# Wavelet attention and mixture of experts on one core: expert 0, the last experts and the shared expert's pieces in another order

## The chip, the cores and the metric

The kernel runs on one core of a Trainium2 chip. The metric is the device time of one execution in microseconds. Five engines work side by side and meet only at semaphores: TensorE (PE; its weight loads are PEld), VectorE (DVE), ScalarE (ACT), GpSimd (POOL) and SyncE (SP), which issues direct DMAs. GpSimd issues the indirect DMAs, gathers and scatters of rows by a list of indices.

## The reference, cut to what matters

Two sequences of 1024 tokens with 128 channels pass a wavelet block with linear attention, and then a mixture of experts:

```python
x = x + attention_block(layernorm(x))           # (2, 1024, 128)
h = layernorm(x).reshape(2048, 128)
scores = sigmoid(h @ gate_w.T)                  # 16 experts
topk_score, topk_ids = top_k(scores.T, 256)     # each expert takes its 256 best tokens
xin = h[topk_ids]
eo = silu(xin @ gw.T + gb) * (xin @ up_w.T + up_b)   # 512 hidden features
eo = eo @ down_w.T + down_b
out = zeros.at[topk_ids].add(eo * topk_score)
shared = (silu(h @ sh_gate_w.T) * (h @ sh_up_w.T)) @ sh_down_w.T   # 256 hidden features
x = x + out + shared
```

## The kernel before, in words

The order of the work is written out by hand, one program for each engine. Nothing plans it at run time: an engine executes its list in order, and each wait on a semaphore stops everything behind it in that list.

**The search.** For each expert the kernel needs the 256th largest score. It finds it in 15 rounds of a search over the bits of the scores (`ROUNDS`). In a round VectorE counts the keys above two candidates (L964), ScalarE those above a third with a Sign (`count_third`, L687), TensorE sums the three counts over partitions (`count`, L1318 to L1322), and VectorE reads the sum (L975) and lays the next candidates (L978). The next round starts from there.

**The shared expert** fills the engines beside the search. Its tokens come in four groups of 512 (`LAST` is group 3). For each group TensorE transposes the features (`features_T`, L1285), multiplies them with four weight tiles (`shared_up`, L1331, gate and up, two each) and, later, multiplies the hidden values with the down weights in four quarters (`shared_down`, L1343, four matmul pairs each group, 16 matmuls of 128 columns in all). ScalarE takes the gate through Silu and copies the up values (`keep_shared`, L700 and L695), copies the transposed features (`keep_hT`, L659) and the down results (`keep_down`, L680). GpSimd multiplies the two halves (L525) and adds the down result of group 0 to `x1` (`shared_add`, L515). Before the change, which piece stands in which round follows from the round's number by a rule, five rounds a group (`PERIOD`): TensorE does a `shared_up` in parts 0 to 3 of a group, with a `shared_down` quarter of the group before, and six warm-up matmuls in part 4; features are transposed in rounds 1, 7 and 11. ScalarE follows one round later (`keep_part`). `stay_warm(n)` issues n matmuls of the identity (L1145), in fp32 two passes each, whose results nobody reads. ScalarE's first Silu stands in round 1, and the compiler puts a load of the activation table ahead of it.

**After the search** the masks become ranks, and VectorE and TensorE turn these into row numbers for four groups of experts: 0 and 1, 2 and 3, 4 to 7 and, `LATE`, 8 to 15. The pieces of the late group's table (`LATER`) are laid between the tiles of the first experts on VectorE. `slot_rows` lets GpSimd gather.

**The experts.** `BLOCKS` lists them: experts 0 to 13 whole (256 tokens, two chunks of 128), experts 14 and 15 in two half blocks each (`HALVED = E - 2`). For step q of block b, with part j of the hidden features (`FT` is 4), TensorE multiplies with the up and the gate weights (L1488 and L1489, an "up" below, two passes each); ScalarE takes the gate through Silu (L745); VectorE makes the hidden tile (L1122); and TensorE multiplies the hidden tile with the down weights (`down`, L1457) two steps later (`LAG`). A block's last down lets VectorE add the bias (`add_bias`, L1104), then ScalarE scale the rows (`weigh`, L571), then GpSimd scatter them (`scatter`, L549). `turn_x` (L1443) transposes the gathered rows of a block, and VectorE copies them (`keep_x`, L1088). For whole blocks the next block's turn stands at part 2 of the block before, while blocks from `HALVED` on are turned late, after the last downs of the block before, with a few warm-ups between (`WARM_B`).

**The order on GpSimd** is fixed: 12 gathers ahead (`AHEAD`), then for each expert two scatters and, after them, two gathers (experts 0 to 5) or one (6 to 13) (`BETWEEN`). Chunk c of the gathers belongs to expert c // 2; so the gather behind expert 9's scatters is expert 13's second, the one behind expert 11's is expert 14's second. An expert's first scatter waits until both scatters of the expert before have landed:

```python
pool.wait_ge(s_scat, 16 * CH * e)      # for e == 0: s_store, the four stores of x1
```

Those stores are issued by SyncE (L399) as soon as a group of `x1` holds the shared expert's part. Group 3's part is added on VectorE by `add_shared(LAST, ...)` (L1055), which needs `shared_down(LAST, ...)`.

**Around expert 0, before.** TensorE's list is: up 0, the row numbers of experts 4 to 7 (`spread(2)`), up 1, `shared_down(LAST)` in four quarters into bank 6, up 2, down 0, turn 1, a wait until bank 6 is read, up 3, down 1, up 4, downs 2 and 3, up 5, up 6, down 4, turn 2, up 7, down 5, up 8. VectorE adds the shared part at step 2, and expert 0's bias at step 4; ScalarE scales expert 0 at step 4.

## Time and profile before

| what | before |
|---|---|
| median of 3 runs | 205.61 us (205.59 to 206.11) |
| the profiled execution | 205.9 us |
| its span, first to last instruction | 204.1 us |
| mean granted TensorE clock | 0.986 of full speed |
| busy: PE, DVE, POOL, ACT | 90%, 64%, 62%, 46% of the span |

The busy shares are averages over stages with different limits. The span is what lies between the first and the last instruction; the execution's own time is 1.8 us longer. In the rows below a time is the start of an instruction in microseconds from the span's start, followed by its duration. "x4" is a merged run of four instructions of one line. In brackets is how long the engine had been idle before, and what ended the idle time; "issue" means that it waited for nothing that the profile shows.

### The profile page before, as it was taken

How to read it: one execution, taken by the hardware profiler on the slowest of the kernel's cores; microseconds unless marked ns; L12 is line 12 of the kernel's file. 1: busy time of each engine (PE TensorE's matmuls, PEld its weight loads, DVE VectorE, ACT ScalarE, POOL GpSimd, SP SyncE). 2: the span in 40 equal slices, each digit the busy share in tenths (PEclk: the TensorE clock that was granted, in tenths of full speed). 3: DMA queues.
4: the chain of work that ended last, by engine and by line, in shares of the span. 5: the costliest groups of instructions: out<-in, count | busy, mean ns of one | idle time of the engine just before them, and what ended most of it. 6: DMA issues, size and time to landing. Idle time of an engine off the chain costs nothing.

```text
span 204.1 us, 3777 instructions
## 1 busy us (share of the span) xinstructions
PE 182.7 (90%) x1246; PEld 157.1 (77%) x1246; DVE 130.3 (64%) x452; ACT 94.2 (46%) x248; POOL 127.3 (62%) x195
## 2 busy tenths in 40 slices
PE   6989889999979999998999999999999979888830
PEld 6957679998936577845998999999999968777720
DVE  4888999999778787887566745544554443434420
ACT  2566612468697768120244244444444442444410
POOL 7598006455117475647766887888877778777550
PEclk9999999999999999999999999999999999999995
DMA  5799999700030271203413322432332233333311
GB/s 173 252 413 419 410 420 412 302 0 3 0 117 0 94 231 51 67 18 109 114 39 51 33 43 42 57 43 35 52 38 33 38 43 40 40 40 39 33 13 13
DMA packets 11652, 22.30 MB, mean 109 GB/s; under 512 B 1504, under 2 KB 8800, under 8 KB 11504
## 3 DMA queue, kind: packets, MB, share of 16 engines
q1 hardware_dynamic: 5968, 17.52, 22.6%
q0 software_dynamic: 5664, 4.53, 16.1%
q8 instruction: 10, 0.16, 0.3%
q14 instruction: 10, 0.08, 0.1%
HBM read 17.72 MB, written 4.33 MB: 108 GB/s over the span
## 4 chain that ended last, share of the span: by engine, by line
PE 38%; POOL 16%; DMA 14%; DVE 12%; issue 10%; ACT 5%; POOLq 1%; SPq 0%; DVEq 0%; ACTq 0%
DMA out_dram<-area,rows 13%; POOL out_dram L549 11%; PE bank L1190 7%; PE bank L1488 4%; PE bank L1331 4%; PE bank L1489 4%; POOL hT L538 3%; PE bank L1457 3%; PE bank L1145 3%; PE bank L1343 2%; POOL rstd L454 2%; DMA x_tok<-in_x_dram 2%; PE bank L1401 1%; PE bank L1293 1%; DVE junk L964 1%
## 5 line engine op out<-in xcount | busy, mean ns | idle before, releaser
L549 POOL DMA_INDIRECT out_dram<-area,rows x32 | 50.6, 1581 | 17.8 <-DMA out_dram<-area,rows 7.2
L1122 DVE SCALAR_TENSOR_TENSOR area<-bank,consts,sgate 128x256 f32<-128x256 f32 (+1 forms) x72 | 32.7, 454 | 44.8 <-ACT sgate L745 44.0
L745 ACT ACTIVATE sgate<-bank,consts 128x256 f32<-128x256 f32 (+1 forms) x72 | 32.4, 450 | 54.8 <-PE bank L1489 54.0
L1488 PE MATMUL bank<-area,wT 128*128 128x256 f32 (+1 forms) x144 | 40.4, 363 | 2.6 <-issue 2.5
L1457 PEld LDWEIGHTS bank<-wT,area 128*128 128x128 f32 x256 | 37.9, 191 | 6.0 <-DVE area L1122 2.7
L1457 PE MATMUL bank<-wT,area 128*128 128x128 f32 x256 | 40.2, 278 | 1.8 <-DVE area L1122 1.8
L538 POOL DMA_INDIRECT hT<-h_rows,rows x32 | 31.7, 991 | 13.3 <-issue 9.2
L1489 PE MATMUL bank<-area,wT 128*128 128x256 f32 (+1 forms) x144 | 39.5, 356 | 0.0
L1489 PEld LDWEIGHTS bank<-area,wT 128*128 128x128 f32 x144 | 26.1, 190 | 2.9
L1488 PEld LDWEIGHTS bank<-area,wT 128*128 128x128 f32 x144 | 21.9, 191 | 4.0 <-issue 3.8
L525 POOL TENSOR_TENSOR sh_hid<-sh_up,sgate 128x64 f32<-128x64 f32 x48 | 13.6, 322 | 15.0 <-ACT sh_up L695 12.4
L1145 PE MATMUL bank<-ident 128*128 128x128 f32 x132 | 19.9, 308 | 1.6 <-POOL ident L418 1.6
L1145 PEld LDWEIGHTS bank<-ident 128*128 128x128 f32 x132 | 18.4, 220 | 1.6 <-POOL ident L418 1.6
L1190 PE MATMUL bank<-sh_hid,area 128*128 128x128 f32 x160 | 18.6, 276 | 0.0
L1190 PEld LDWEIGHTS bank<-sh_hid,area 128*128 128x128 f32 x160 | 18.2, 192 | 0.3 <-ACT area L618 0.3
L1331 PE MATMUL bank<-hT,sh_wT 128*128 128x512 f32 x32 | 17.6, 636 | 0.6 <-ACT hT L659 0.6
L571 ACT ACTIVATE area<-area,hT 128x128 f32<-128x128 f32 x32 | 11.2, 392 | 7.9 <-DVE area L1104 7.9
L964 DVE TENSOR_SCALAR_CACHE_REDUCE junk<-area,search 128x256 bf16<-128x256 f32 (+1 forms) x30 | 13.2, 477 | 1.3 <-ACT area L673 0.8
L1343 PEld LDWEIGHTS bank<-sh_wT,sh_hid 128*128 128x128 f32 x64 | 8.5, 191 | 4.1 <-issue 2.9
L454 POOL TENSOR_TENSOR rstd<-var_eps,half_pow 128x4 f32<-128x4 f32 (+1 forms) x6 | 7.4, 1230 | 6.1 <-DVE var_eps L775 6.1
L498 POOL TENSOR_TENSOR x_tok<-x_tok,consts 128x128 f32<-128x128 f32 x4 | 3.1, 814 | 12.4 <-DVE area L887 12.4
L687 ACT ACTIVATE below<-area,search 128x256 bf16<-128x256 f32 (+1 forms) x15 | 7.6, 509 | 4.8 <-DVE search L978 4.0
(197 smaller groups left out, 265.5 us busy)
## 6 DMA issues: line engine op xcount, KB each, us to landing
wT<-in_weights_dram SPq DMA_DIRECT2D x16, 768.0 KB, 16.5
h_rows<-hrow SPq DMA_DIRECT2D x2, 576.0 KB, 3.7
x_tok<-in_x_dram SPq DMA_DIRECT2D x4, 256.0 KB, 3.6
x_tok<-in_down_b_dram SPq DMA_DIRECT2D x1, 1024.0 KB, 6.4
out_dram<-x SPq DMA_DIRECT2D x4, 256.0 KB, 2.2
hT<-h_rows,rows POOLq DMA_INDIRECT x32, 2.6
out_dram<-area,rows POOLq DMA_INDIRECT x32, 3.3
sh_wT<-in_shared_dram SPq DMA_DIRECT2D x1, 384.0 KB, 3.0
```

What stands on the lines that cost most here:

```text
L525: last = pool.tensor_tensor(sh_hid[:, n % 2, t, k:k + 64], sh_up[:, t, k:k + 64], sgate[:, t, k:k + 64], ALU.mult)
L538: pool.indirect_dma_start(out=gath[:, e % GBUF, c, :], out_offset=None, in_=h_rows[:, :], in_offset=bass.IndirectOffsetOnAxis(ap=rows[:, c ...
L549: pool.indirect_dma_start(out=out_rows, in_=eo[:, e % EOB, c, :], in_offset=None, out_offset=bass.IndirectOffsetOnAxis(ap=rows[:, c, e:e + ...
L745: act.activation(sgate_e[:, q % SGB, 0:n], up_bank(q)[:, CAP:CAP + n], ACT.Silu, bias=biasT[:, 1, j, e:e + 1]).then_inc(s_sil, 1)
L964: last = dve.tensor_scalar(junk[:, k, :], keys, cand[:, k:k + 1], 0.0, ALU.is_ge, ALU.add, accum_out=cnt[:, k:k + 1])
L1122: dve.scalar_tensor_tensor(hidden[:, b % 2, j, 0:n], up_bank(q)[:, 0:n], biasT[:, 0, j, e:e + 1], sgate_e[:, q % SGB, 0:n], ALU.add, ALU.m ...
L1145: pe.matmul(spare[:, 0:P], ident[:, :], ident[:, :], start=True, stop=True)
L1190: last = pe.matmul(dst, band[:, b, m0 + o:m0 + o + P], diag_c[:, d0 - 4 + k, :], start=False, stop=(d0 == 4 and o == 2), skip_group_check= ...
L1331: pe.matmul(bank[2 * kind + t][:, :], sh_wT[:, 2 * kind + t, :], rhs, start=True, stop=True).then_inc((s_shg, s_shu)[kind], 1)
L1457: last = pe.matmul(bank[3 + b % 2][:, i * P:(i + 1) * P], hidden[:, b % 2, j, i * P:(i + 1) * P], wT[:, e, 2, j, :], start=(j == 0 and i = ...
L1488: pe.matmul(up_bank(q)[:, 0:n], wT[:, e, 0, j, :], xselT[:, b % 2, 0:n], start=True, stop=True)
L1489: pe.matmul(up_bank(q)[:, CAP:CAP + n], wT[:, e, 1, j, :], xselT[:, b % 2, 0:n], start=True, stop=True).then_inc(s_gu, 1)
```

## The change

`HALVED` becomes E - 1: expert 14 is a whole block and only expert 15 is halved. A new constant, `TURN_LATE`, keeps the late turn, the late bias add and the late scaling for blocks from 14 on. The warm-ups ahead of the late blocks are now five before expert 14 and none before the two halves of expert 15; before, they were two ahead of each of the last three half blocks.

Expert 0's last three downs are issued at step 3. Group 3's `shared_down` moves from ahead of up 2 to a place between down 1 and down 2 and goes to bank 4; VectorE adds it at the end of step 3, directly ahead of expert 0's bias, and ScalarE scales expert 0 at step 3, ahead of the Silu of step 4.

In the search, tables by round take the place of the rule. TensorE's first `shared_up` stands in round 1, and no round holds more than one `shared_up` with one other piece. ScalarE's first Silu of the shared expert moves to round 2, and an 8-column Silu into a new tile `idle` stands in round 1. Warm-ups in the search are 15 in seven rounds, where they were 18 in three.

```diff
-    HALVED = E - 2
+    HALVED = E - 1
+    TURN_LATE = E - 2
+        idle = sb("idle", [P, 8])
         ROUNDS = [b for b in range(BITS - LOW - 2, -1, -2)] + [b for b in range(LOW - 2, -1, -2)]
         PERIOD = 5
+        ACT_PARTS = {2: (0, 0), 3: (0, 1), 4: (0, 2), 5: (0, 3), 6: (1, 0), 7: (1, 1), 8: (1, 2), 9: (1, 3),
+                     11: (2, 0), 12: (2, 1), 13: (2, 2), 14: (2, 3)}
+        UP_PARTS = {1: (0, 0, 0), 2: (0, 0, 1), 3: (0, 1, 0), 4: (0, 1, 1), 5: (1, 0, 0), 6: (1, 0, 1), 7: (1, 1, 0),
+                    8: (1, 1, 1), 10: (2, 0, 0), 11: (2, 0, 1), 12: (2, 1, 0), 13: (2, 1, 1)}
+        DOWN_PARTS = {7: ((0, 0),), 8: ((0, 1),), 9: ((0, 2), (0, 3)), 11: ((1, 0),), 12: ((1, 1),), 13: ((1, 2),),
+                      14: ((1, 3),)}
+        TURN_PARTS = {2: 1, 5: 2, 10: 3}
+        WARM_PARTS = {0: 3, 1: 2, 3: 2, 4: 2, 6: 2, 9: 1, 14: 3}
...
-        WARM_B = {HALVED + 1: 2, HALVED + 2: 2, HALVED + 3: 2}
+        WARM_B = {TURN_LATE: 5}
...
# ScalarE, round r of the search
-                if r:
-                    keep_part(r - 1)
-                if r == 2:
-                    keep_hT(1)
+                if r == 1:
+                    act.activation(idle[:, :], ident[:, 0:8], ACT.Silu)
+                if r in ACT_PARTS:
+                    keep_shared(*ACT_PARTS[r])
+                if r == 3:
+                    keep_hT(1)
+                if r == 10:
+                    keep_down(0)
...
-            keep_part(len(ROUNDS) - 1)
+            keep_down(1)
...
# ScalarE, step q of the experts
-                if b >= HALVED and j == 0:
+                if b >= TURN_LATE and j == 0:
                     weigh(act, b - 1)
...
-                if q == FT or j == 2 and 1 < b < HALVED:
+                if q == FT - 1:
+                    weigh(act, 0)
+                elif j == 2 and 1 < b < TURN_LATE:
                     weigh(act, b - 1)
...
# VectorE, step q
-                if q == 2:
-                    add_shared(LAST, bank[6])
-                if b >= HALVED and j == 0:
+                if b >= TURN_LATE and j == 0:
...
-                if q == FT or j == 1 and 1 < b < HALVED:
+                if q == FT - 1:
+                    add_shared(LAST, bank[4])
+                    add_bias(0)
+                elif j == 1 and 1 < b < TURN_LATE:
                     add_bias(b - 1)
...
# TensorE, shared_down of the last group
                 else:
                     pe.wait_ge(s_lasthid, SHT)
+                    pe.wait_ge(s_lastbase, 1)
...
# TensorE, round r
-                n, part = divmod(r, PERIOD)
-                if n < LAST and part < 4:
-                    shared_up(n, part // 2, part % 2)
-                    if n:
-                        shared_down(n - 1, part)
-                if part == 4:
-                    stay_warm(WARM_S, bank[6 + n % 2])
-                if r in (1, 7, 11):
-                    features_T(1 + r // 4)
+                if r in UP_PARTS:
+                    shared_up(*UP_PARTS[r])
+                for part in DOWN_PARTS.get(r, ()):
+                    shared_down(*part)
+                if r in TURN_PARTS:
+                    features_T(TURN_PARTS[r])
+                stay_warm(WARM_PARTS.get(r, 0), bank[6] if r in (3, 4) else bank[7])
...
# TensorE, step q
                 if q == 2:
-                    for t in range(4):
-                        shared_down(LAST, t)
-                if q == 3:
-                    pe.wait_ge(s_lastbase, 2)
+                    pe.wait_ge(s_lasthid, SHT)
...
-                if q == FT:
+                if q == FT - 1:
                     down(q - LAG)
+                    for t in range(4):
+                        shared_down(LAST, t)
                     down(q - 1)
-                elif q >= LAG and q != FT + 1 and not (b >= HALVED and j < LAG):
+                    down(q)
+                elif q >= LAG and not ((b == 1 or b >= TURN_LATE) and j < LAG):
+                    if q == FT + LAG:
+                        pe.wait_ge(s_lastbase, 2)
                     down(q - LAG)
...
-                if j == 2 and b + 1 < HALVED:
+                if j == 2 and b + 1 < TURN_LATE:
                     turn_x(b + 1)
```

## Rows read from the trace of the kernel before

**Rows 1.** The page's chain that ended last: shares of the span by line.

```profile
DMA out_dram<-area,rows 13%; POOL out_dram L549 11%; PE bank L1190 7%; PE bank L1488 4%; PE bank L1331 4%; PE bank L1489 4%; POOL hT L538 3%; PE bank L1457 3%; PE bank L1145 3%; PE bank L1343 2%; POOL rstd L454 2%; DMA x_tok<-in_x_dram 2%; PE bank L1401 1%; PE bank L1293 1%; DVE junk L964 1%
```

**Rows 2.** Timeline of GpSimd: start, duration, engine, line, operation [idle before, releaser].

```profile
74.65 1.70 POOL L515 TENSOR_TENSOR x<-sh_down,x 128x128 f32<-128x128 f32 x4
...
105.34 1.62 POOL L549 DMA_INDIRECT out_dram<-area,rows  x1 [1.49 <-ACT area L571]
...
112.66 1.61 POOL L549 DMA_INDIRECT out_dram<-area,rows  x1 [1.23 <-ACT area L571]
...
119.13 1.61 POOL L549 DMA_INDIRECT out_dram<-area,rows  x1 [0.35 <-issue]
...
164.86 1.02 POOL L538 DMA_INDIRECT hT<-h_rows,rows  x1 [0.30 <-issue]
...
175.61 1.02 POOL L538 DMA_INDIRECT hT<-h_rows,rows  x1 [0.30 <-issue]
...
196.96 1.55 POOL L549 DMA_INDIRECT out_dram<-area,rows  x1 [1.73 <-ACT area L571]
```

**Rows 3.** Timeline of VectorE in the search: rounds 1, 2, 8, 9 and 11.

```profile
58.09 0.16 DVE L975 TENSOR_SCALAR_CACHE_REDUCE search<-bank 128x3 f32<-128x3 f32 x1 [0.43 <-PE bank L1322]
...
60.07 0.16 DVE L975 TENSOR_SCALAR_CACHE_REDUCE search<-bank 128x3 f32<-128x3 f32 x1 [0.62 <-PE bank L1322]
...
70.81 0.16 DVE L975 TENSOR_SCALAR_CACHE_REDUCE search<-bank 128x3 f32<-128x3 f32 x1 [0.54 <-PE bank L1322]
...
72.47 0.16 DVE L975 TENSOR_SCALAR_CACHE_REDUCE search<-bank 128x3 f32<-128x3 f32 x1 [0.29 <-PE bank L1322]
...
75.97 0.40 DVE L978 SCALAR_TENSOR_TENSOR search<-search 128x3 f32<-128x3 f32 x1
```

**Rows 4.** Timeline of ScalarE: an 8-column activation, the table load, round 2's Sign.

```profile
2.09 0.21 ACT L602 ACTIVATE diag<-ident 128x8 f32<-128x8 f32 x1
...
57.31 1.28 ACT L700 ACT_TABLE_LOAD   x1
...
59.10 0.50 ACT L687 ACTIVATE below<-area,search 128x256 bf16<-128x256 uint16 x1
```

**Rows 5.** Chain of waits around expert 0 on TensorE: start, share of the chain in us.

```profile
96.94 1.78 PE bank L1343 x16
...
100.26 0.43 PE bank L1488 x2
```

**Rows 6.** Timeline of VectorE around expert 0.

```profile
98.77 0.69 DVE L1055 TENSOR_TENSOR x<-bank,x 128x512 f32<-128x512 f32 x1 [0.79 <-PE bank L1343]
...
103.63 0.41 DVE L1104 TENSOR_TENSOR area<-bank,x_tok 128x256 f32<-128x256 f32 x1
...
105.24 0.48 DVE L1122 SCALAR_TENSOR_TENSOR area<-bank,consts,sgate 128x256 f32<-128x256 f32 x1 [0.86 <-ACT sgate L745]
...
106.82 0.42 DVE L1088 COPY area<-bank 128x256 f32<-128x256 f32 x1
```

**Rows 7.** The page's DMA issues: count, KB each, median us from issue to landing.

```profile
out_dram<-x SPq DMA_DIRECT2D x4, 256.0 KB, 2.2
```

**Rows 8.** Timeline of TensorE ahead of and in the last experts.

```profile
168.69 0.44 PE L1443 MATMUL bank<-ident,hT 128*128 128x128 f32 x2 [1.37 <-DMA hT<-h_rows,rows]
...
174.21 0.60 PE L1488 MATMUL bank<-area,wT 128*128 128x256 f32 x2
...
176.87 0.27 PE L1443 MATMUL bank<-ident,hT 128*128 128x128 f32 x1
...
177.79 0.46 PE L1488 MATMUL bank<-area,wT 128*128 128x128 f32 x2 [0.65 <-issue]
...
181.42 0.61 PE L1145 MATMUL bank<-ident 128*128 128x128 f32 x4
...
182.57 0.46 PE L1488 MATMUL bank<-area,wT 128*128 128x128 f32 x2 [0.43 <-issue]
```

**Rows 9.** The page's 40 slices: granted TensorE clock in tenths of full speed.

```profile
PEclk9999999999999999999999999999999999999995
```

More of the change, by code:

```diff
@@ L700, in keep_shared @@
                 act.activation(sgate[:, t, :], bank[t][:, :], ACT.Silu).then_inc(s_shsil, 1)
-            def keep_part(r):
-                n, part = divmod(r, PERIOD)
-                if part < 4:
-                    keep_shared(n, part)
-                elif n:
-                    keep_down(n - 1)
             for r in range(len(ROUNDS)):
@@ L1298, in _ @@
             WARM_1 = 10
-            WARM_I, WARM_S, WARM_L, WARM_C = 2, 6, 3, 4
+            WARM_I, WARM_L, WARM_C = 2, 3, 4
             pe.wait_ge(s_gc, 1)
@@ L1342, in shared_down @@
                 for k in range(SHT):
-                    last = pe.matmul(bank[6 if n == LAST else 4][:, t * P:(t + 1) * P], sh_hid[:, n % 2, k, t * P:(t + 1) * P], sh_wT[:, 4 + k, :],
+                    last = pe.matmul(bank[4][:, t * P:(t + 1) * P], sh_hid[:, n % 2, k, t * P:(t + 1) * P], sh_wT[:, 4 + k, :],
                                      start=(k == 0), stop=(k == SHT - 1))
@@ L1352, in _ @@
                 count(r + 1)
-                n, part = divmod(r, PERIOD)
-                if n < LAST and part < 4:
-                    shared_up(n, part // 2, part % 2)
-                    if n:
-                        shared_down(n - 1, part)
-                if part == 4:
-                    stay_warm(WARM_S, bank[6 + n % 2])
-                if r in (1, 7, 11):
-                    features_T(1 + r // 4)
+                if r in UP_PARTS:
[5 more added lines that the diff above has]
+                stay_warm(WARM_PARTS.get(r, 0), bank[6] if r in (3, 4) else bank[7])
             for k in range(2):
@@ L1466, in _ @@
                 n = len(chunks) * P
-                if b >= HALVED and j == 0:
+                if b >= TURN_LATE and j == 0:
                     down(q - LAG)
@@ L1499, in _ @@
                     spread(LATE)
-                if j == 2 and b + 1 < HALVED:
+                if j == 2 and b + 1 < TURN_LATE:
                     turn_x(b + 1)
```

## The prediction

> **What bounds the kernel now.** I read the chain of waits first, then the timelines of VectorE, ScalarE, TensorE and GpSimd. In the chain, by line, the expert scatters (DMA 13% and GpSimd 11%) lead, and TensorE lines follow in small shares [rows 1]: no single engine sets the end. It is a relay. The search is paced by VectorE reading a count each round. From the first scatter the GpSimd queue sets the pace: scatter, scatter, one or two gathers, 6.4 us a round (119.13 less 112.66) [rows 2], and it is held only where an expert's output is late. At the end TensorE leads again: the last scatter idled 1.73 us for ScalarE's scaling [rows 2]. What the change is worth is read from these three places.
>
> **The search's rounds.** VectorE's idle time before it reads the count is 0.29 in an undisturbed round; it is 0.43 in round 1, 0.62 in round 2, 0.54 in round 8 [rows 3]. In round 1 TensorE still runs a shared matmul put into round 0. The change puts nothing but warm-up there: 0.14 saved. In round 2 ScalarE's table load (57.31, 1.28 us) and a 512-column Silu delay the Sign to 59.10 [rows 4]. Now an 8-column Silu carries the load. An 8-column activation takes 0.21 [rows 4]; consecutive ones overlap by 0.1 (58.59 plus 0.60 would be 59.20, the Sign starts at 59.10), so the Sign starts at 58.70. It is 0.39 earlier while the round begins 0.14 earlier, so of the 0.33 excess 0.08 stays: 0.25 saved. In round 8 TensorE came late because round 7 held an up matmul pair, a down quarter and a transpose of features; no new round holds three. 0.25 saved. Sum 0.64, off everything behind the search.
>
> The new rounds hold at most an up with one other piece, or an up with two warm-ups. The warm-ups cost nothing, being over before the next count; that they go down from 18 to 15 costs nothing while the clock holds. If a new round ran over, 0.3 of the sum would go, by the excess of rows of round 2 or 8; the upper end is 0.64 plus 0.08 plus the following 0.24.
>
> In round 11 a three-column update on VectorE took 0.40, where other three-column rows take 0.16, while GpSimd added the shared expert's rows, 74.65 to 76.35 [rows 2, 3]. I leave these 0.24 us in: GpSimd's work hangs on pieces of rounds 9 and 10, which ScalarE copies in the same rounds as before.
>
> The Trainium skill (SBUF — State Buffer, Who interferes with whom) says that a VectorE instruction with two SBUF inputs and a GpSimd one that reads SBUF exclude each other; by that rule every such update beside GpSimd's work could stretch like this one. The trace agrees for that row. If GpSimd's work were moved by a round, the sum would gain or lose about 0.24 each time.
>
> **Expert 0.** Before, the last shared_down (16 matmuls, 1.78) stood ahead of up 2, and expert 0's last downs after up 4. An up pair is 0.87 (0.43 twice), a down a quarter of the 1.78, 0.45 [rows 5], a turn of two passes 0.22 (half of the four passes below). With up 2 in shared_down's place (from 96.94): down 0 at 97.81, turn 98.25, up 3 at 98.47, down 1 at 99.34, shared_down 99.79 to 101.57, downs 2 and 3 to 102.46, ups 4 to 6 from there. VectorE adds the shared rows at 101.6 instead of 98.77, and expert 0's bias 0.12 after the downs, about 102.6, instead of 103.63 [rows 6]. Behind the add wait, on VectorE, the bias add, hidden tile 4 and the pieces of the late table; on SP the fourth store, which the first scatter waits for. Issued at 102.3, when the 0.69 of the add are over, with 2.2 to landing [rows 7] and 0.3 to 0.5 of GpSimd's start, after an issue of some 0.4, it lets the scatter go at 105.2 to 105.4, against 105.34: that gain is swallowed by the store. It costs nothing either, while the next scatter, one round of 6.4 later (111.6 to 111.8), is not earlier than its own data.
>
> That data is expert 1's, and this decides. Scatter 1 idled 1.23 for ScalarE, until 112.66 [rows 2]. Expert 2's first up (and so expert 1's last downs) waits for VectorE's copy at 106.82. Before, hidden tile 5 followed the bias add by 1.61, and the copy followed that tile by 1.58 [rows 6]. Now it is tile 4 that queues behind expert 0's scaling: 102.6 plus 1.61 is 104.2, one more tile with its table piece 0.80, plus 1.58: 106.56. So expert 1, and with it the whole GpSimd queue, gains 0.26. Bounds: 0 (same work on VectorE) and 0.93 (the 1.23, less the 0.30 which GpSimd always idles between two issues).
>
> **The last experts.** Expert 14 becomes whole, so one late turn goes, but it now needs both its gathers. The second is issued at 175.61. Expert 13's second was issued at 164.86 and TensorE started on it at 168.69: 3.83 [rows 2, 8]. So the turn comes at 179.44; before, the first half turned at 176.87. The first up followed the turn by 0.92 [rows 8]; with a 256-column copy (0.42) in place of one of 128 I take 0.98: 180.42. Three ups and a down lie before the last up: 3.06. From expert 13's last up (174.21) to the next block's first (177.79) are 3.58 [rows 8]. So 15a starts at 187.06. A half block takes 4.78 (182.57 less 177.79), of which the two warm-ups, four passes or 0.45 on TensorE (0.61 less one pass's 0.27, over three, times four) [rows 8] and partly beside the bias add, were about 0.30 (bounds 0 and 0.45); they are removed there. 15b starts at 191.54. Before, it started at 182.57 plus two half blocks, 192.13, and the last scatter came 4.83 later. So the end moves 0.59. Bounds: minus 0.7, no gain from the warm-ups and a gather later by a microsecond, which I chose; plus 1.43, the 1.73 less 0.30, where the GpSimd queue itself becomes the bound. The last gather would land at about 190.2 (two queue rounds of 5.38 after 175.61, plus 3.83), just before 15b's turn wants it.
>
> **Sum.** 0.64 + 0.26 + 0.59 = 1.49. The profiled execution took 205.9 (span 204.1), 0.29 above the median of the runs, 205.61. From 205.9 comes 204.4; against the median 204.1, 0.7% faster. About 0.3% (0.62 us) is what a measurement of this kernel can tell from no change.
>
> **Rivals.**
> *The queue follows expert 0.* If expert 1 came as early as expert 0, both idle times (1.49 and 1.23, less 0.30 each: 2.12) would go: 205.61 - 0.64 - 2.12 - 0.59 = 202.3. For it: the rows name ScalarE as what both waited for. Against: VectorE's copy, and the store. 10%.
> *Expert 14's second gather is late.* One more microsecond of landing is one microsecond at the end: 205.1. For it: the gather stands behind a scatter in the same queue. Against: the 3.83 was taken in the same position. 17%.
> *The rounds keep their length*, since another engine ends them: 204.1 + 0.64 = 204.7. For it: in round 2 three engines end within tenths. Against: the excess shows up only in named rounds. 13%.
> *TensorE's clock falls*, the slower case. Before expert 14 TensorE has nothing from the end of five warm-ups (176.9 plus 1.2) to 179.4. If the granted clock then went to 1.2 GHz, expert 14's four ups and four downs, 5.3, would take twice as long: 209.4. It decides from 2.1 us of work at that clock (1.49 + 0.62). Against: TensorE idled 1.37 before 168.69 [rows 8] and the clock stayed in its top tenth, the 2.4 GHz level, in every slice but the last [rows 9]. 6%.
>
> The Trainium skill (TensorE: Matmul & The Clock Gate, HAM oscillation — how this bites in real kernels) tells of kernels whose waits for DMA throw TensorE back to the lower clock; by that rule this late turn would be such a place. The trace does not bear it out for the idle time of 1.37.
>
> **Chances.** The forecast, 52%, has its own range of 203.5 to 204.7; 2% are left for the rest. Below 205.0 lie the forecast, the first rival, nearly all of the third and half of the second: faster 0.80. Within 0.3%: 0.13. Slower: 0.07. The range from 202.7 to 205.2 takes in the bounds of the search and of the head and most of the late gather, and leaves out part of the first rival and the clock.
>
> **What would show it.** After: idle before the count near 0.29 in rounds 1 and 8 and near 0.37 in round 2, and everything behind the search 0.64 earlier: expert 0's bias add near 102.0, first scatter still released late, near 104.6; scatter 1 near 111.8, still after ScalarE. TensorE waits for a gather before expert 14 (near 178.5), and the last scatter starts near 195.5, behind ScalarE. It is wrong if scatter 1 comes below 111.2, if no wait for a gather stands before expert 14, or if a new round of the search shows an idle of 0.5.

## The result, and the profile after the change

In 20 executions each, the changed kernel took 204.59 us (median; 204.02 to 207.16), the kernel before 205.81 (205.46 to 208.13). The ratio is 0.993, with a 95% interval of 0.9906 to 0.9954: faster by 0.5 to 0.9%. The forecast was 0.7% and 204.1 us, so the total came out near the forecast (1.22 us by the medians, for 1.49). Its parts did not, and that is what the experiments are about. (Medians here are over all executions; ratios compare undisturbed executions only, so the two can differ, here by up to half a per cent.)

The changed kernel was profiled in two sessions. The rows below are from the second, called `whole` in the experiments: execution 204.5, span 202.8, against 205.9 and 204.1 before. Lines have moved: L983 and L986 are the count read and the update that were L975 and L978; L697 is the Sign, L710 and L719 the Silus, L1451 the turn, L1493 and L1494 an up pair, L1465 a down, L1128 the hidden tile, L1112 the bias add, L1096 VectorE's copy, L581 the scaling, L548 a gather, L559 a scatter.

**The search.** The timeline of VectorE, the reads of the count in rounds 1, 2 and 8, and round 11's update (start, us, then the idle time before it and who ended it):

```profile
57.75 0.16 DVE L983 TENSOR_SCALAR_CACHE_REDUCE search<-bank 128x3 f32<-128x3 f32 x1 [0.29 <-PE bank L1331]
59.50 0.16 DVE L983 TENSOR_SCALAR_CACHE_REDUCE search<-bank 128x3 f32<-128x3 f32 x1 [0.39 <-PE bank L1331]
...
69.94 0.16 DVE L983 TENSOR_SCALAR_CACHE_REDUCE search<-bank 128x3 f32<-128x3 f32 x1 [0.24 <-PE bank L1331]
...
75.11 0.45 DVE L986 SCALAR_TENSOR_TENSOR search<-search 128x3 f32<-128x3 f32 x1
```

The idle times of 0.43, 0.62 and 0.54 [rows 3] have fallen to 0.29, 0.39 and 0.24. ScalarE's timeline in the same profile shows why in round 2: the Sign starts at 58.53, not at 59.10 [rows 4].

```profile
57.12 1.28 ACT L719 ACT_TABLE_LOAD   x1
58.41 0.21 ACT L719 ACTIVATE idle<-ident 128x8 f32<-128x8 f32 x1
58.53 0.49 ACT L697 ACTIVATE below<-area,search 128x256 bf16<-128x256 uint16 x1
```

**Expert 0.** TensorE's timeline: the third table, then expert 0's turn. Before, the turn followed the table at 93.26 without a wait; now it waits:

```profile
91.41 0.77 PE L1409 MATMUL bank<-area 128*64 128x64 f16 x16
92.83 0.44 PE L1451 MATMUL bank<-ident,hT 128*128 128x128 f32 x2 [0.65 <-DMA hT<-h_rows,rows]
```

VectorE's timeline, expert 0's bias add and the copy that expert 2 waits for (103.63 and 106.82 in [rows 6]):

```profile
102.07 0.42 DVE L1112 TENSOR_TENSOR area<-bank,x_tok 128x256 f32<-128x256 f32 x1 [0.20 <-PE bank L1465]
...
106.11 0.42 DVE L1096 COPY area<-bank 128x256 f32<-128x256 f32 x1
```

**The queue and the end.** GpSimd's timeline: expert 0's two gathers, the first scatters of experts 0 and 1, the second gather of expert 14, and the last four scatters:

```profile
87.78 1.16 POOL L548 DMA_INDIRECT hT<-h_rows,rows  x1 [3.72 <-DVE rows L1057]
89.25 0.95 POOL L548 DMA_INDIRECT hT<-h_rows,rows  x1 [0.30 <-issue]
...
104.34 1.65 POOL L559 DMA_INDIRECT out_dram<-area,rows  x1 [1.63 <-DMA out_dram<-x]
...
111.96 1.61 POOL L559 DMA_INDIRECT out_dram<-area,rows  x1 [1.49 <-ACT area L581]
...
175.17 1.02 POOL L548 DMA_INDIRECT hT<-h_rows,rows  x1 [0.30 <-issue]
...
187.60 1.58 POOL L559 DMA_INDIRECT out_dram<-area,rows  x1 [0.66 <-DMA out_dram<-area,rows]
189.49 1.56 POOL L559 DMA_INDIRECT out_dram<-area,rows  x1 [0.30 <-issue]
193.76 1.55 POOL L559 DMA_INDIRECT out_dram<-area,rows  x1 [2.72 <-DMA out_dram<-area,rows]
195.62 1.55 POOL L559 DMA_INDIRECT out_dram<-area,rows  x1 [0.30 <-issue]
```

The last scatter no longer idles 1.73 for ScalarE [rows 2]; it follows its neighbour. TensorE's timeline ahead of experts 13 and 14, and ScalarE's last scaling:

```profile
168.29 0.44 PE L1451 MATMUL bank<-ident,hT 128*128 128x128 f32 x2 [1.67 <-DMA hT<-h_rows,rows]
...
176.46 1.28 PE L1154 MATMUL bank<-ident 128*128 128x128 f32 x10
177.85 0.44 PE L1451 MATMUL bank<-ident,hT 128*128 128x128 f32 x2
```

```profile
194.13 0.40 ACT L581 ACTIVATE area<-area,hT 128x128 f32<-128x128 f32 x1 [1.29 <-DVE area L1112]
```

How much earlier each point comes than before, in these two profiles:

| point | before | after | earlier by |
|---|---|---|---|
| round 0's count read | 56.29 | 56.10 | 0.19 |
| last count read (round 14) | 81.18 | 80.14 | 1.04 |
| first gather | 88.93 | 87.78 | 1.15 |
| turn of expert 0 | 93.26 | 92.83 | 0.43 |
| first scatter | 105.34 | 104.34 | 1.00 |
| scatter of expert 1 | 112.66 | 111.96 | 0.70 |
| scatter of expert 14 | 188.27 | 187.60 | 0.67 |
| last scatter but one | 193.68 | 193.76 | -0.08 |
| last scatter | 196.96 | 195.62 | 1.34 |

The 0.19 of the first row is no work of the change: the search has not begun to differ there, and `last_alone` (below), whose search is that of the kernel before, reads this count at 56.05. It is in every row. Behind it 0.7 is lost between the first gather and the turn, another 0.75 between expert 14's scatters and the next one, and 1.4 is won between the last two scatters.

### The profile page after: what moved, and what is told of

It is laid out like the page before. It is cut to its first block, busy times and chain, and to the rows that moved or that the text cites. A ratio compares the mean times of both kernels' runs of the same rounds, so it can differ in the third digit from the quotient of the medians.

```text
span 205.4 us, 3712 instructions
## 1 busy us (share of the span) xinstructions
PE 184.5 (90%) x1222; PEld 158.4 (77%) x1222; DVE 128.9 (63%) x446; ACT 93.0 (45%) x245; POOL 127.3 (62%) x195
## 4 chain that ended last, share of the span: by engine, by line
PE 40%; DMA 16%; POOL 14%; DVE 11%; issue 9%; ACT 5%; POOLq 1%; SPq 0%; DVEq 0%; ACTq 0%
POOL out_dram L559 10%; DMA out_dram<-area,rows 10%; PE bank L1199 7%; PE bank L1493 6%; PE bank L1494 5%; PE bank L1340 5%; PE bank L1465 4%; DMA hT<-h_rows,rows 4%; POOL hT L548 4%; DMA x_tok<-in_x_dram 2%; PE bank L1353 2%; PE bank L1154 2%; PE bank L1302 1%; DVE junk L972 1%; DVE area L829 1%
## 5 line engine op out<-in xcount | busy, mean ns | idle before, releaser
L559 POOL DMA_INDIRECT out_dram<-area,rows x32 | 50.6, 1583 | 20.2 <-DMA out_dram<-area,rows 6.7
L1128 DVE SCALAR_TENSOR_TENSOR area<-bank,consts,sgate 128x256 f32<-128x256 f32 (+1 forms) x68 | 31.8, 468 | 46.6 <-ACT sgate L751 46.2
L751 ACT ACTIVATE sgate<-bank,consts 128x256 f32<-128x256 f32 (+1 forms) x68 | 31.3, 461 | 57.0 <-PE bank L1494 56.7
L1493 PE MATMUL bank<-area,wT 128*128 128x256 f32 (+1 forms) x136 | 41.3, 387 | 2.3 <-issue 2.3
L1465 PEld LDWEIGHTS bank<-wT,area 128*128 128x128 f32 x256 | 38.4, 194 | 5.3 <-DVE area L1128 1.9
L1465 PE MATMUL bank<-wT,area 128*128 128x128 f32 x256 | 39.8, 279 | 1.2 <-DVE area L1128 1.2
L1494 PE MATMUL bank<-area,wT 128*128 128x256 f32 (+1 forms) x136 | 40.2, 379 | 0.0
L548 POOL DMA_INDIRECT hT<-h_rows,rows x32 | 31.6, 989 | 13.2 <-issue 9.2
L1494 PEld LDWEIGHTS bank<-area,wT 128*128 128x128 f32 x136 | 26.4, 198 | 3.6
L1493 PEld LDWEIGHTS bank<-area,wT 128*128 128x128 f32 x136 | 21.7, 197 | 3.7 <-issue 3.3
L1154 PEld LDWEIGHTS bank<-ident 128*128 128x128 f32 x124 | 17.8, 220 | 3.5 <-issue 1.9
L1154 PE MATMUL bank<-ident 128*128 128x128 f32 x124 | 19.1, 307 | 1.6 <-POOL ident L428 1.6
L581 ACT ACTIVATE area<-area,hT 128x128 f32<-128x128 f32 x32 | 11.0, 391 | 9.3 <-DVE area L1112 9.3
L697 ACT ACTIVATE below<-area,search 128x256 bf16<-128x256 f32 (+1 forms) x15 | 7.6, 506 | 4.3 <-DVE search L986 3.4
```

The lines of the kernel that those rows point to most:

```text
L548: pool.indirect_dma_start(out=gath[:, e % GBUF, c, :], out_offset=None, in_=h_rows[:, :], in_offset=bass.IndirectOffsetOnAxis(ap=rows[:, c ...
L559: pool.indirect_dma_start(out=out_rows, in_=eo[:, e % EOB, c, :], in_offset=None, out_offset=bass.IndirectOffsetOnAxis(ap=rows[:, c, e:e + ...
L751: act.activation(sgate_e[:, q % SGB, 0:n], up_bank(q)[:, CAP:CAP + n], ACT.Silu, bias=biasT[:, 1, j, e:e + 1]).then_inc(s_sil, 1)
L1128: dve.scalar_tensor_tensor(hidden[:, b % 2, j, 0:n], up_bank(q)[:, 0:n], biasT[:, 0, j, e:e + 1], sgate_e[:, q % SGB, 0:n], ALU.add, ALU.m ...
L1154: pe.matmul(spare[:, 0:P], ident[:, :], ident[:, :], start=True, stop=True)
L1465: last = pe.matmul(bank[3 + b % 2][:, i * P:(i + 1) * P], hidden[:, b % 2, j, i * P:(i + 1) * P], wT[:, e, 2, j, :], start=(j == 0 and i = ...
```

## The experiments

### The three parts, each alone

The whole change once more, and each part put into the kernel before by itself. `search_alone` takes the new tables for the rounds; `expert0_alone` the new places of shared_down, expert 0's downs, its bias add and scaling; `last_alone` only this:

```diff
-    HALVED = E - 2
+    HALVED = E - 1
+    TURN_LATE = E - 2
-        WARM_B = {HALVED + 1: 2, HALVED + 2: 2, HALVED + 3: 2}
+        WARM_B = {TURN_LATE: 5}
-                if b >= HALVED and j == 0:
+                if b >= TURN_LATE and j == 0:
...
```

> The whole change once more, for a profile without the two falls of TensorE's granted clock that the first one shows (0.50 of full speed at 96 to 99 us and at 171 to 174 us). Theory (three gains in a relay, each on the path): 1.3 to 1.6 us faster than before; in the profile the first gather about 1.0 earlier than before, scatter 1 another 0.2 to 0.3 earlier, TensorE waiting for a gather ahead of expert 14 near 178.5, and the last scatter behind ScalarE near 195.5. Rival (the search alone gives the gain and the rest is swallowed): about 0.9 faster, with the last scatter near 196.0.

> Only the shared expert's pieces are laid anew over the search's rounds; expert 0 and the last experts stay as before. Theory: everything behind the search moves by the same amount, 0.6 (the forecast's sum) to 1.0 (the first profile after: 0.9 from the first round to the masks), so the time falls by that. Rival (something behind the search absorbs it, for instance the stores of x1 or the gathers): less than 0.4.

> Only expert 0's re-ordering; the search and the last experts stay as before. Theory (scatter 1 hangs on expert 1, which hangs on VectorE's copy for expert 2): 0.1 to 0.4 faster, the first scatter not earlier than 105.0 and ended by the fourth store, scatter 1 still behind ScalarE. Rival (the queue follows expert 0): 1.5 to 2.1 faster. Second rival (the store now holds the whole queue back): 0.2 to 0.6 slower.

> Only the last experts: expert 14 whole, turned late, five warm-ups ahead of it and none ahead of the halves of 15. Theory (the second gather of expert 14 sets its start): 0.3 to 0.7 faster, TensorE waiting for a gather until about 179.4. Rival (the late gather eats the gain): 0 or up to 0.5 slower. Other rival (GpSimd's queue is the bound, not TensorE): 1.2 to 1.4 faster.

Measured, against 205.86 before:

| kernel | median | ratio | 95% interval |
|---|---|---|---|
| whole | 204.63 | 0.9943 | 0.9904 to 0.9981 |
| search_alone | 207.23 | 1.0048 | 1.0011 to 1.0084 |
| expert0_alone | 205.59 | 0.9982 | 0.9951 to 1.0014 |
| last_alone | 204.64 | 0.9942 | 0.9905 to 0.9978 |

The last experts alone are as fast as the whole. They were expected to give 0.3 to 0.7 us and gave 1.2, as the rival in which GpSimd's queue is the bound had it. `whole` itself gave 1.2 for 1.3 to 1.6 expected, and `expert0_alone` fell where it was expected, 0.1 to 0.4, but is not clear of no change. The search alone was expected 0.6 to 1.0 faster; it is slower than before, although its rounds are as short as in `whole`. Its profile: the second gather on GpSimd, TensorE's turn of expert 0 and a later up, then stretches of 1 us (busy time and count per engine; the granted clock, DMA share and GB/s end the line), then the first scatter.

```profile
89.36 0.95 POOL L547 DMA_INDIRECT hT<-h_rows,rows  x1 [0.30 <-issue]
...
93.36 0.44 PE L1446 MATMUL bank<-ident,hT 128*128 128x128 f32 x2 [1.07 <-DMA hT<-h_rows,rows]
...
95.92 1.22 PE L1491 MATMUL bank<-area,wT 128*128 128x256 f32 x2
```

```profile
92.00:93.00 1.00, 0.29 (x8) 0.18 (x6) 0.40 (x1) 0.00 (x0) 0.81 (x1) 1.00 0.34 78
93.00:94.00 1.00, 0.44 (x2) 0.20 (x2) 0.16 (x1) 0.00 (x0) 0.88 (x1) 1.00 0.67 211
...
96.00:97.00 1.00, 1.00 (x3) 0.82 (x4) 0.56 (x2) 0.00 (x0) 0.70 (x2) 0.50 0.28 74
```

```profile
107.09 1.62 POOL L558 DMA_INDIRECT out_dram<-area,rows  x1 [4.27 <-ACT area L580]
```

The gather that was issued at 89.36 landed 4.0 us later. TensorE, busy 0.29 and 0.44 in the two stretches, then had a granted clock of 0.50, which is 1.2 GHz, and the two up passes at 95.92 took 1.22, twice their time. The wait eats the search's gain: the turn comes at 93.36, for 93.26 before. The clock costs the rest: from the turn to expert 1's scatter 21.05 passed, for 19.40 before. The first session's profile of the changed kernel shows the same (a wait of 0.74, clock 0.50 from 96 to 99); that of `whole` has the wait but not the clock. In all three the gather was issued near 89.3; in `before`, `expert0_alone` and `last_alone`, where it was issued 1 us later, nothing waited, and in the last two it landed in 2.5. Why should an earlier gather be slower?

### What lies in the gather's way

The view of DMA, 90 to 92 in `whole`: 40 slices of 0.05 us, the busy share in tenths and GB/s, and a queue of instructions, q8.

```profile
DMA  0000000000000090099399000000000060000000
GB/s 0 0 0 0 0 0 0 0 0 0 0 0 0 0 328 0 0 184 461 92 276 369 0 0 0 0 0 0 0 0 0 0 92 0 0 0 0 0 0 0
q8 instruction: 1, 0.02, 2.9%
```

A packet of 16 KB of queue q8 is put down to the slice at 90.70, and took 0.93 us of one engine (2.9% of 16 engines over 2 us). The second gather's rows move from 90.85 to 91.10, all but one slice's worth of 92 GB/s (4.6 KB, a sixteenth of the gather's 0.07 MB), which comes at 91.60, when the packet is over (90.70 plus 0.93). The gather counts as landed only with it: fifteen of the sixteen parts of its landing were in by 91.77, the last at 92.78. The same view of `before` has this packet at 89.0, ahead of the rows of all gathers. No row names the engine whose instructions q8 brings. By the count it is TensorE: the page of `before` has ten packets of q8 and 2,492 matmul passes and weight loads, 249 to a packet (196 to 300 between one packet and the next), and no other engine has more than 452 instructions. Where the packet falls should then hang on how many instructions TensorE has had: the change has fewer there (15 warm-ups for 18), and all other work comes earlier.

The Trainium skill (Runtime: NRT & Kernel Launch, Instruction fetch mechanics) says that each engine's sequencer refills its instructions in blocks of 16 KiB, 256 instructions, over a DMA queue of its own, and calls that mostly hidden. The size and the average count agree with these rows. No wait of TensorE is put down to the packet here, but the gather beside it is held back.

The kernel before has such a meeting too. DMA, 166 to 168 in `before`, where expert 13's second gather (issued at 164.86 [rows 2]) moves:

```profile
DMA  0000000000093799300000000000000050000000
GB/s 0 0 0 0 0 0 0 0 0 0 0 788 92 184 276 276 92 0 0 0 0 0 0 0 0 0 0 0 0 0 0 0 92 0 0 0 0 0 0 0
...
q8 instruction: 1, 0.02, 3.4%
```

The packet stands at 166.55 with 1.09 us, and the last sixteenth comes at 167.60. This is the gather whose 3.83 us the prediction took as the time from issue to use.

It holds far beyond these two. In the 14 profiles, 396 gathers have a landing on record. 36 of them took over 3.2 us, up to 4.5, and a packet of q8 began 0.4 to 2.5 us after the issue of every one. For 31 it began 1.2 to 2.2 us after the issue; among the other 360 gathers there is none with a packet in that stretch.

### Moving the packet and nothing else

`whole_early` and `search_early` put 30 instructions more ahead of expert 0, in about the same time:

```diff
-                stay_warm(WARM_PARTS.get(r, 0), bank[6] if r in (3, 4) else bank[7])
+                if r in (1, 3, 4):
+                    stay_warm_small(9, bank[6] if r in (3, 4) else bank[7])
+                else:
+                    stay_warm(WARM_PARTS.get(r, 0), bank[7])
...
+            def stay_warm_small(n, spare):
+                for _ in range(n):
+                    pe.matmul(spare[0:32, 0:32], ident_b[:, 0:32], ident_b[:, 0:32], start=True, stop=True)
```

`before_late` takes 48 out of the kernel before, to bring its packet onto its gather:

```diff
-                    stay_warm(WARM_S, bank[6 + n % 2])
+                    pe.matmul(bank[6 + n % 2][:, :], ident[:, :], hT[:, 0:4, :].rearrange("p i t -> p (i t)"), start=True, stop=True)
+                    stay_warm(1, bank[6 + n % 2])
```

`no_search` is the whole change with the rounds of before. A rival to the packet is that an early gather is slow in itself, wherever the packet is.

> The changed kernel with three pairs of warm-up matmuls of search rounds 1, 3 and 4 (8 instructions a pair) replaced by 9 small ones each (18 instructions, about the same time): 30 instructions more in TensorE's stream ahead of expert 0, no other edit. Theory 'instruction fetch': in the changed kernel the 16 KB instruction packet of TensorE's queue moves at 90.7 and takes 0.93 us of one DMA engine, while the second gather's rows (90.6 to 91.1) move, and that gather lands 3.5 us after its issue instead of 2.5. With 30 instructions more the packet moves near 88.7, the gather lands 2.5 to 2.7 us after its issue, expert 0's transposes start at 92.1 right behind the third table instead of 92.83 with 0.65 of waiting, no granted clock of 0.50 shows at 95 to 99, and the median is 203.6 to 204.1 against 204.63 of the change as made. Rival 'early gathers are slow in themselves' (they land late because they are issued at 89.2): the wait stays at 0.6 to 1.1 and the median stays at 204.4 to 204.9.

> The search's part of the change alone, with the same 30 instructions more in TensorE's stream. Theory 'instruction fetch': the gather lands in 2.5 to 2.7 us, expert 0's transposes start near 92.2 instead of 93.36, the granted clock stays at 1.00 there, and the median falls from 207.23 to 204.9 to 205.4, 0.5 to 1.0 under the kernel before. Rival 'early gathers are slow in themselves': the wait of about 1.07 stays, and the median stays over 206.

> The kernel before with each of its three groups of six warm-up matmuls (rounds 4, 9, 14) replaced by one of 512 columns and one of 128: 48 instructions fewer in TensorE's stream, and nothing else. Theory 'instruction fetch': the packet that moved at 89.0, before any gather, now moves near 92, on the rows of the second gather (92.0 to 92.4), so this gather lands 3.4 to 4 us after its issue instead of 2.5, expert 0's transposes, which waited for nothing at 93.26, wait 0.5 to 1.1 us, and the kernel is 0.4 to 1.2 us slower than the kernel before, more where the granted clock falls behind the wait. Rival: where the packet moves is of no account; the transposes start at 93.3 and the time is within 0.2 us of the kernel before.

> The change without its search part: expert 0's turn and the last experts as in the changed kernel, the search's rounds as before. Theory 'the search's gain is lost at expert 0's turn': expert 0's part is worth 0.3 and the last experts' 1.2, sum 204.1 to 204.5, so it is as fast as the whole change (204.63) or faster. Rival 'the search's part is worth its 0.64 in the whole change': this kernel is 0.5 to 0.7 slower than the whole change, 205.1 to 205.4.

Measured, against 206.07 before:

| kernel | median | ratio | 95% interval |
|---|---|---|---|
| whole_early | 204.87 | 0.9915 | 0.9878 to 0.9953 |
| search_early | 205.11 | 0.9921 | 0.9886 to 0.9957 |
| before_late | 208.15 | 1.0051 | 1.0005 to 1.0097 |
| no_search | 204.72 | 0.992 | 0.9889 to 0.9952 |

`search_early` against `search_alone` is the clearest: the same search, 30 instructions apart, 0.8% faster than before instead of 0.5% slower, and the intervals don't touch. Its median is where it was expected, 204.9 to 205.4. In both early kernels the turn follows the table without a wait. `whole_early`: the second gather, the turn, and DMA from 90 to 92, where no part of the gather is left behind. The gather is issued as early as in `whole` (89.25) and lands in 2.5, for 3.5 there, so it is not slow for being early:

```profile
89.42 0.95 POOL L548 DMA_INDIRECT hT<-h_rows,rows  x1 [0.30 <-issue]
...
92.29 0.44 PE L1460 MATMUL bank<-ident,hT 128*128 128x128 f32 x2
```

```profile
DMA  2500000000000000000009999600000000000000
GB/s 92 184 0 0 0 0 0 0 0 0 0 0 0 0 0 0 0 0 0 0 0 461 184 369 276 184 0 0 0 0 0 0 0 0 0 0 0 0 0 0
```

`before_late` is the converse, slower by 1.05 us by the ratio (2.1 by the medians), for 0.4 to 1.2 expected, and just clear of no change. TensorE at expert 0 and, at the tail, at expert 13; a stretch behind the first; DMA from 92 to 94:

```profile
94.09 0.44 PE L1444 MATMUL bank<-ident,hT 128*128 128x128 f32 x2 [0.82 <-DMA hT<-h_rows,rows]
...
169.69 0.44 PE L1444 MATMUL bank<-ident,hT 128*128 128x128 f32 x2
```

```profile
96.00:98.00 2.00, 2.00 (x6) 1.28 (x5) 0.66 (x2) 0.47 (x1) 1.39 (x3) 0.50 0.16 39
```

```profile
DMA  8798200000000000000040003993962020000000
GB/s 184 184 369 276 92 0 0 1 0 0 0 0 0 0 0 0 0 0 0 0 92 0 0 0 92 369 276 92 276 184 92 0 92 0 0 0 0 0 0 0
```

The packet, now at 91.9 with 1.06 us, holds a sixteenth of the gather back until 93.0; the turn waits 0.82, and the granted clock, 1.00 until then, falls to 0.50. From the turn to expert 1's scatter 20.80 passed, for 19.40 in `before`, and in `search_early`, where nothing waited. At the tail the packet left its old place (it is now at 173.4): expert 13's gather landed in 2.6 instead of 3.8, and the 1.37 of waiting of [rows 8] is gone. There it hits a scatter instead:

```profile
170.71 1.56 POOL L549 DMA_INDIRECT out_dram<-area,rows  x1 [0.30 <-issue]
172.57 1.02 POOL L538 DMA_INDIRECT hT<-h_rows,rows  x1 [0.30 <-issue]
175.70 1.58 POOL L549 DMA_INDIRECT out_dram<-area,rows  x1 [2.11 <-DMA out_dram<-area,rows]
```

A wait of 2.11 where its neighbours have 0.6 to 0.8, since each expert's first scatter waits for the landing of the last one's second. `whole_early` paid in the same coin: its last packet, of 1.50 us, moved from 191.1 to 186.0, and a wait of 0.7 became 2.25:

```profile
183.68 1.55 POOL L559 DMA_INDIRECT out_dram<-area,rows  x1 [0.31 <-issue]
...
188.81 1.58 POOL L559 DMA_INDIRECT out_dram<-area,rows  x1 [2.25 <-DMA out_dram<-area,rows]
```

Its median missed the 203.6 to 204.1 expected, though the turn came as expected; this one profile shows a wait that can account for it. `no_search` missed its 204.1 to 204.5 by 0.2, but not 205.1 to 205.4, the rival's: without its search part the change is as fast as with it.

### Other places, and the table load

`whole_p18` and `whole_p54` are `whole_early` with 7 and 13 small matmuls for 9. `whole_noidle` leaves the 8-column Silu out of the changed kernel:

```diff
-                if r == 1:
-                    act.activation(idle[:, :], ident[:, 0:8], ACT.Silu)
```

> The changed kernel with 18 instructions more in TensorE's stream (rounds 1, 3 and 4 hold 7 small warm-up matmuls each in place of 2 large ones). Theory 'instruction fetch, wherever it falls': a 16 KB packet of TensorE's queue costs time where it moves beside a transfer that something waits for, and nothing elsewhere. With 18 more the front packet moves near 89, so expert 0's transposes start behind the third table without a wait, and the last packet, at 191.0 in the changed kernel (where the last wait for a scatter was 2.72) and at 185.9 with 30 more (where a wait was 2.25 in place of 0.66), moves near 188 to 189.5, beside the issue of a scatter, where the kernel before had it and lost nothing. Then the last-but-one scatter idles 2.0 to 2.2 and the time is 203.2 to 204.0. Rival: the packets' places at the tail are of no account, and the time is that of the changed kernel, 204.4 to 204.9.

> The same with 54 instructions more (13 small matmuls in place of 2 large ones in each of the three rounds). Theory 'instruction fetch, wherever it falls': the front packet near 86, well ahead of the gathers; the tail packets near 163 and 183 to 184, beside the issue of a scatter, so no wait of over 1 us for a scatter before the last pair; 203.2 to 204.0. If the last packet lands again behind the second scatter of a pair (3.3 to 4.8 us after the first of the pair starts) one wait of 1.5 to 2.3 shows there and the time stays at 204.4 to 205. Rival: places of no account, 204.4 to 204.9 and no such wait whatever the place.

> The changed kernel without the 8-column Silu of round 1, so that the table load falls to the 512-column Silu of round 2 as in the kernel before. By the working of the forecast the count of round 2 then comes 0.2 to 0.3 later (its idle time 0.6 to 0.7 in place of 0.39), and all behind it. Rival 'the table load is hidden either way': idle 0.4, no difference.

Against 205.88 before: `whole_p18` 204.50, ratio 0.9919 (0.9884 to 0.9954); `whole_p54` 204.86, 0.9951 (0.9922 to 0.9981). Both missed 203.2 to 204.0. Yet executions of `whole_p18` lie in two groups, four at 203.3 to 204.0 and five at 204.5 to 205.2, and the profiled one, 203.76, shows what an execution of the lower group looks like: no wait at expert 0, and none of over 1 us for a scatter's landing before the last pair, though the last packet went to 186.3, not to 188.

```profile
92.17 0.44 PE L1460 MATMUL bank<-ident,hT 128*128 128x128 f32 x2
```

```profile
187.09 1.58 POOL L559 DMA_INDIRECT out_dram<-area,rows  x1 [0.70 <-DMA out_dram<-area,rows]
```

The packet stood there 0.3 us later than in `whole_early`, whose profiled execution, 205.11, is of the upper kind. The places can be moved but not set: 18, 30 and 54 instructions all brought this packet to 186.0 to 186.3.

`whole_noidle`: 205.92 in 8 widely scattered executions, 0.995 (0.9909 to 0.9991), not to be told from the change. Its profile answers the question. ScalarE's table load, and VectorE's count reads of rounds 2 and 3:

```profile
58.88 1.28 ACT L710 ACT_TABLE_LOAD   x1
60.17 0.60 ACT L710 ACTIVATE sgate<-bank 128x512 f32<-128x512 f32 x1
```

```profile
59.50 0.16 DVE L981 TENSOR_SCALAR_CACHE_REDUCE search<-bank 128x3 f32<-128x3 f32 x1 [0.29 <-PE bank L1329]
61.64 0.16 DVE L981 TENSOR_SCALAR_CACHE_REDUCE search<-bank 128x3 f32<-128x3 f32 x1 [0.77 <-PE bank L1329]
```

The load shows, one round later than expected: round 3 idles 0.48 more, round 2 0.10 less. The small Silu is worth 0.38 to the search, against 0.25 in the forecast. This profile also has the packet on the second gather, at 91.3: it landed in 3.75, the turn waited 0.87, and the clock was 0.50 from 95.0 to 98.4.

### The gap ahead of the search

In the profiles of `no_search` and `search_early`, not in the others, the granted clock fell to 0.50 near 49.8, behind a place where TensorE waits for ScalarE's copy of x1. A stretch of `no_search`:

```profile
50.00:50.50 0.50, 0.50 (x4) 0.50 (x4) 0.47 (x2) 0.50 (x2) 0.14 (x1) 0.50 0.16 33
```

Everything behind it came 1.6 to 1.9 later. `whole_p18_gap` fills the place and keeps 18 instructions more:

```diff
                 turn_x1(g)
+                stay_warm(WARM_G[g], bank[5])
                 router(g - 1)
+            WARM_G = (0, 0, 2, 0)
```

> The changed kernel with the front packet moved (again 18 instructions more ahead of expert 0: 8 in the two added matmuls, 10 by the small ones of rounds 1, 3 and 4), and two warm-up matmuls in the place where TensorE waits for ScalarE's copy of x1 (48.1 to 48.6). In two profiles (the change without its search part, and the search's part with 30 instructions more) the granted clock was 0.50 from about 49.8 to 53 behind that place, and all behind it came 1.4 to 1.7 later; in the profiles of the other kernels, with the same gap, it stayed at 1.00. Theory 'the gap decides it, by chance from one execution to the next': the executions of about 205.0 to 205.2 of the kernel with 18 more go, and the median falls from 204.50 to 203.3 to 203.9. Rival 'the upper executions come from a wait behind expert 0 or at the tail': the spread of 203.3 to 205.2 stays and the median stays at 204.0 to 204.9.

It took 204.79, against 205.72 before; ratio 0.9909 (0.9874 to 0.9945). The two groups stayed, five executions at 203.3 to 204.0 and seven at 204.8 to 205.5, so the gap does not make them. The rival holds in that the spread stayed. What makes the upper group is not shown: the execution that was profiled, 203.39, is of the lower, with neither a wait at expert 0 nor one of over 1 us for a scatter's landing before the last pair. That a packet meets a scatter in some executions, as in `whole_early`'s profile, fits, but is only argued.

## Why the prediction was right, and where it was not

The total held: 0.7% was forecast, 0.7% measured, and the range took the median in. The steps behind it held only in part:

- **Search, 0.64: right in the rounds, wrong behind them.** From round 0's to round 14's count read 0.85 was won: 0.15 in round 1, 0.23 in round 2, 0.30 in round 8 (0.14, 0.25 and 0.25 forecast), and 0.17 in rounds 12 to 14, which the forecast had not counted, nearly all from round 12's update (0.16 instead of 0.30). Round 11's stayed, 0.45, as forecast. The step that failed is "0.64, off everything behind the search": at expert 0's turn 0.43 was left, 0.19 of it from ahead of the search, since the gather landed 3.5 us after its issue. By itself this part made the kernel slower.
- **Expert 0, 0.26: right.** From the turn (0.43 earlier) to the scatter of expert 1 (0.70 earlier) 0.27 was won. It is no chance: 19.40 passed there in `before`, `last_alone` and `search_early`, 19.13 in `whole`, `expert0_alone`, `no_search` and `whole_early`. The bias add at 102.07 and the copy at 106.11 stand near the forecast's 102.0 and, less 0.64, 105.9 (the forecast's terms for the copy, as printed, add up to 106.59, not 106.56, a gain of 0.23); the first scatter waits for the fourth store at 104.34, as forecast. By its time alone this part's gain, 0.2%, cannot be told from none.
- **Last experts, 0.59: mis-sized.** The term was built on "3.83" from issue to use of the gather. That row was itself a gather behind an instruction packet. In `last_alone` TensorE turned expert 14 at 178.12, 2.6 us after the issue at 175.50 and right behind the warm-ups, not at 179.44; 15a started at 185.81, not at 187.06. ScalarE's last scaling came 1.89 earlier in `last_alone` (194.39 for 196.28). What ended the gain was the upper bound given: "plus 1.43 ... where the GpSimd queue itself becomes the bound". The distance between the last two scatters fell from 3.28 to 1.86, by 1.42. By the forecast's own test, "no wait for a gather stands before expert 14", this step was wrong, and the end came at 195.62 behind GpSimd's own scatter, not behind ScalarE.
- **What came back.** Between the second scatter of expert 14 and the next, 4.27 passed instead of 3.53, since the second landed late. In `whole` fourteen of the sixteen parts of its landing were in by 192.72, the last two at 193.37 and 193.50, and two packets began beside its rows: one of q8 at 191.08 (1.23 us) and one of 8 KB of another instruction queue, q14, at 191.75 (0.78 us). In `whole_p18` q8's was long past and only one of q14 stood there, at 191.54; one part came late, at 192.72 after 192.30, and 4.00 passed. In `whole_early`, with no packet beside the rows, 3.65 passed and no part came late. So packets account for it here too, but no run moved q14's alone.
- **The rivals.** "The queue follows expert 0" did not come: scatter 1 still waited for ScalarE, until 111.96. "The rounds keep their length" did not come: 0.85 was won in them. "TensorE's clock falls" did, in some executions only, and not before expert 14: behind expert 0's wait, and in the first session's profile also behind a wait of 1.94 ahead of expert 13. "Expert 14's second gather is late" was the opposite of what happened.

In sum, the forecast was 0.64 + 0.26 + 0.59, or 1.49. The profiles gave 0.19 that no edit made, 0.24 from the search, 0.27 and 1.42, less 0.75 at the last landing and 0.03 in the queue: 1.34 at the last scatter. That the total was right is luck: the search's part came 0.40 short and 0.75 came back, while the last experts' term was 0.83 too small. Instruction packets stand behind all three.

The Trainium skill (TensorE: Matmul & The Clock Gate, HAM oscillation — how this bites in real kernels) tells of waits for DMA that throw TensorE back to the lower clock. The forecast held that the trace spoke against it; at expert 0 the profiles of `search_alone` and `before_late` agree with it, with waits of 1.07 and 0.82, while `whole`, with 0.65, kept its clock, and kept it over the 1.67 ahead of expert 13 too.

No version is shown to beat the change: `whole_p18` has the lowest executions, 203.3 against 204.0, but the intervals overlap.

## What to carry to other kernels

A row's duration is a price only if nothing met it there: before a gather's 3.8 us is used as a term, look at what other gathers of the profile take (a median of 2.6 here) and at the DMA view of that moment. Where work depends on small transfers, adding or removing instructions on an engine moves its instruction packets, and an edit that costs nothing by its own can gain or lose a microsecond far behind it, as 30 instructions did in `search_early`; so test a part with a few instructions more or less before judging it. And follow a gain to the next thing that waits for something else: the search's 0.85 was lost at a gather 9 us behind it.

## What the runs showed of the hardware that was not expected

- A 16 KB instruction packet (TensorE's, by the count of instructions to a packet and since it moved when TensorE's count changed) took 0.9 to 1.6 us of one DMA engine, and a sixteenth of an indirect transfer came only behind it: expert 0's second gather took 3.5 to 4.0 us instead of 2.5, and waits for a scatter of 0.6 to 0.8 became 2.1 to 2.5.
- The same sparse stretch on TensorE leads to the lower granted clock in one execution and not in another: near 49.8 in two of the profiles, behind expert 0 with a wait of 0.74 in one session's profile and not with 0.65 in the next one's.
